# Attention products of 128 output channels issued as two column halves of 64, in a float32 stack of attentions and scans

## Chip, core and metric
The kernel runs on one NeuronCore of one Trainium2 chip. The metric is the device time of one execution in microseconds (us), inputs and output in device memory.

## What is computed
The input x is 4 images of 512 channels on 16 x 16 positions, float32. Four layers follow each other, each added to its own input; the input of a layer is group-normalised first (32 groups of 16 channels).

```python
# layers 0 and 2: attention over the 256 positions of an image
e1 = relu(w1 @ xf + b1); e2 = relu(w2 @ xf + b2)          # 64 channels each
assembly = relu(w3 @ xf + b3)                             # 512 channels
attn = softmax(e1.T @ e2)                                 # 256 x 256
y = alpha * (xf @ attn.T) + assembly
# layer 1 (PReLU) and layer 3 (ReLU): a scan along one image axis, forth and back
cur = act(Wc @ prev + b) + x_i                            # Wc 512 x 512, 64 columns
...
x = x + layer(group_norm(x))
```

## The kernel before
The 512 channels lie as K = 4 chunks of 128 partitions. Everything is float32, apart from some bfloat16 products of zeros that keep TensorE's clock up. The program is written per engine, with semaphores by hand, so the order of the instructions in the code is the order on each engine.

**Attention** (`attention` in TensorE's program, line 309) goes through four images one after the other. For each image TensorE issues, in this order:
- the embeddings of both branches at once (L330): 4 products, weights 128 x 128, on the 256 positions;
- in layer 2 only, 8 transposes of the normalised image, 128 x 128 (L338);
- the ReLU branch `relu_branch` (L318), output chunk m = 0 (and one product of m = 1 in layer 0), 4 products a chunk;
- the scores (L353): 2 products with 64 rows each, one on the lower and one on the upper 64 rows of the array;
- in the first and in the last image of an attention the product for group means of the norm to come (L299), behind the scores;
- the ReLU branch's chunk 1, then in the first and last image the product for group variances (L306), then chunk 2 (and one product of chunk 3 in layer 0);
- 4 transposes of the probabilities (L370), and the rest of the ReLU branch's chunk 3;
- the output (L383): 8 products, weights 128 x 128, on 256 positions, two for each output chunk.

ScalarE makes the embeddings (L467, L469), the exponentials and the ReLU branch's results out of the PSUM banks; VectorE finds the maximum, scales the probabilities, adds the residual (L668 or L671) and writes the new image (L685 or L688), and takes its statistics (L580). The three kinds of waits ahead of products are for embeddings (L350), probabilities (L367) and copied transposes (L379).

**Scans** (`scan_step`, L397) have 30 steps each. In a step 16 products of 128 x 128 weights go on 64 columns; each is issued as two products of 64 output channels (TILE = 64, L408), the first with its output on PSUM partitions 0 to 63 and the second on 64 to 127. Outside the scans, all weights with 128 output channels are used whole.

Around an attention, `critical_norm` (L437) issues the products of zeros (L290) and the group products while VectorE and GpSimd work out the norm.

Of the kernel before, what the change touches and what calls it, by code (L numbers as in the profile page):

```python
# [20 lines left out]
P = 128  # L21
N = 4
C = 512
K = C // P
T = 16
POS = T * T
PC = POS // P
# [25 lines left out]
TILE = 64  # L53
# [66 lines left out]
def preact_stack(nc, a):  # L120
    with ExitStack() as ctx:
        def sb(name, shape, dt=F32):
            return ctx.enter_context(nc.sbuf_tensor(name, shape, dt))
# [5 lines left out]
        bank = [banks[:, b] for b in range(8)]  # L129
# [10 lines left out]
        w12 = {l: sb(f"w12_{l}", [P, K, 2 * D]) for l in (0, 2)}  # L140
        w3 = {l: sb(f"w3_{l}", [P, K, C]) for l in (0, 2)}
# [22 lines left out]
        xn = [sb(f"xn{s}", [P, K, POS]) for s in range(2)]  # L164
# [5 lines left out]
        probT = sb("probT", [P, PC, POS])  # L170
# [71 lines left out]
        def images(engine, image):  # L242
            image(0, 0, first=True)
            with engine.Fori(0, (N - 2) // 2) as pair:
                image(pair * 2 + 1, 1)
                image(pair * 2 + 2, 0)
            image(N - 1, 1, last=True)
# [3 lines left out]
        def o_bank(m):  # L251
            return bank[(4, 7, 5, 6)[m]][:, 0:POS]
# [33 lines left out]
        def _(pe):  # L286
# [6 lines left out]
            def group_means(l, r):  # L293
                s = norm[l]
                c0, c1 = norm_rounds(l)[r]
                pe.wait_ge(s.stats, c1)
                if l == 0 and r == 0:
                    pe.wait_ge(s_gavg, 16)
                nc.tensor.matmul(bank[4][:, 0:(c1 - c0) * SETS], gavg[:], st[:, c0:c1, :, 1],  # L299
                                 start=True, stop=True).then_inc(s.mean, 1)  # L300

            def group_variances(l, r):
                s = norm[l]
                c0, c1 = norm_rounds(l)[r]
                pe.wait_ge(s.vadd, r + 1)
                nc.tensor.matmul(bank[5][:, 0:(c1 - c0) * SETS], gavg[:], vadd[:, c0:c1],  # L306
                                 start=True, stop=True).then_inc(s.var, 1)

            def attention(l):
                s = att[l]  # L310
                if l == 0:
                    pe.wait_ge(s_w12[l], 16)
                else:
                    pe.wait_ge(s_signed12, K)

                def relu_branch(xn_s, m, done, ks=range(K)):
                    for k in ks:
                        mm = nc.tensor.matmul(bank[2 + m // 2][:, m % 2 * POS:(m % 2 + 1) * POS],  # L318
                                              w3[l][:, k, m * P:(m + 1) * P], xn_s[:, k],
                                              start=(k == 0), stop=(k == K - 1))  # L320
                    if done:
                        mm.then_inc(s.a_mm, 1)

                if l == 0:
                    pe.wait_ge(s_small, 32)

                def image(n, h, first=False, last=False):
                    for k in range(K):
                        pe.wait_ge(s.xn_ready, n * K + k + 1)
                        mm = nc.tensor.matmul(bank[1][:, 0:POS], w12[l][:, k], xn[h][:, k],  # L330
                                              start=(k == 0), stop=(k == K - 1))
                    mm.then_inc(s.e_mm, 1)
                    if not first:
                        pe.wait_ge(s.x_done, n * K)
                    if l == 2:
                        for pc in range(PC):
                            for k in range(K):
                                mm = nc.tensor.transpose(bank[6 + pc][:, k * P:(k + 1) * P],  # L338
                                                         xn[h][:, k, pc * P:(pc + 1) * P], ident[:])
                            mm.then_inc(s.xnT_mm, 1)  # L340
                    if first:
                        if l == 0:
                            pe.wait_ge(s_w3[l], 16)
                        else:
                            pe.wait_ge(s_signed3, K)

                    ahead = 1 if l == 0 else 0
                    relu_branch(xn[h], 0, False)
                    relu_branch(xn[h], 1, False, range(ahead))
                    pe.wait_ge(s.e_ready, (n + 1) * 4)  # L350
                    for ic in range(PC):
                        rows = slice(ic * D, (ic + 1) * D)
                        mm = nc.tensor.matmul(scores[:, ic * POS:(ic + 1) * POS],  # L353
                                              e1[rows, ic * P:(ic + 1) * P], e2[rows], start=True, stop=True)
                    mm.then_inc(s.s_mm, 1)
                    if first:
                        group_means(l, 1)
                    if last:
                        group_means(l + 1, 0)
                    relu_branch(xn[h], 1, True, range(ahead, K))  # L360
                    if first:
                        group_variances(l, 1)
                    if last:
                        group_variances(l + 1, 0)
                    relu_branch(xn[h], 2, False)
                    relu_branch(xn[h], 3, False, range(ahead))
                    pe.wait_ge(s.p_ready, (n + 1) * PC)  # L367
                    for jc in range(PC):
                        for ic in range(PC):
                            mm = nc.tensor.transpose(bank[1 - jc][:, ic * P:(ic + 1) * P],  # L370
                                                     prob[:, ic, jc * P:(jc + 1) * P], ident[:])
                        mm.then_inc(s.pt_mm, 1)
                    relu_branch(xn[h], 3, True, range(ahead, K))
                    if l == 0:
                        pe.wait_ge(s_xT[n], 16)
                    else:
                        pe.wait_ge(s.xnT_copied, (n + 1) * PC)

                    pe.wait_ge(s.pt_copied, (n + 1) * PC)  # L379
                    by_position = xT[:, n] if l == 0 else xnT  # L380
                    for m in range(K):
                        for jc in range(PC):
                            mm = nc.tensor.matmul(o_bank(m),  # L383
                                                  by_position[:, jc, m * P:(m + 1) * P], probT[:, jc],
                                                  start=(jc == 0), stop=(jc == PC - 1))
                        mm.then_inc(s.o_mm, 1)
                        if m == 1:
                            pe.wait_ge(s.r_ready, (n + 1) * K)

                if l == 0:  # L390
                    for n in range(N):
                        image(n, n % 2, first=n == 0, last=n == N - 1)
                else:
                    images(pe, image)
# [50 lines left out]
            for l in range(0, 4, 2):  # L445
                critical_norm(l, 0)
                attention(l)
                critical_norm(l + 1, 1)
                if l == 0:
                    clear_banks()  # L450
                    prelu_scan()
                else:
                    relu_scan()
# [555 lines left out]
```

## Time and profile before

| | us |
|---|---|
| median of 3 runs | 268.09 |
| lowest, highest | 267.37, 268.49 |
| the profiled execution | 268.07 |
| its span, first to last instruction | 266.3 |
| TensorE matmul busy | 255.9 (96%) |
| TensorE weight load busy | 220.5 (83%) |
| VectorE busy | 174.6 (66%) |
| ScalarE busy | 94.2 (35%) |
| GpSimd busy | 66.2 (25%) |

The first attention runs from about 10 to 67 us of the span, the first scan from 72 to 139, the second attention from 145 to 202 and the second scan from 207 to 264. PE is TensorE's matmul, PEld its weight load, which can run beside it. Matmuls are pipelined, so the mean duration of one is longer than the distance between two; the busy time of a group of back-to-back matmuls, divided by their number, gives the distance. A float32 product shows as two MATMUL and two LDWEIGHTS records, each called a pass here.

### The profile page before, as it was taken

The page shows a single profiled execution, that of the slowest core. Times are in us where ns is not written, and L with a number is a line of the kernel's source. Part 1 is how long each engine was busy: PE and PEld are TensorE (multiplying, and loading weights), DVE is VectorE, ACT ScalarE, POOL GpSimd, SP SyncE. Part 2 cuts the span into 40 slices and gives each one's busy share as a digit, 9 for nine tenths or more (in the row PEclk, how much of TensorE's full clock was granted, in tenths as well). Part 3 has the DMA queues.
Part 4 walks back from the last instruction along what each step waited for, and adds up shares of the span by engine and source line. Part 5 has one row for each costly group of instructions (what it writes and reads, how often), then busy time and mean ns, then how long its engine had stood idle before and what let it go on. Part 6 is the DMA issues. An engine that isn't in the chain of part 4 may idle for free.

```text
span 266.3 us, 10980 instructions
## 1 busy us (share of the span) xinstructions
PE 255.9 (96%) x4480; PEld 220.5 (83%) x4480; DVE 174.6 (66%) x656; ACT 94.2 (35%) x225; POOL 66.2 (25%) x100
## 2 busy tenths in 40 slices
PE   8799999999879999999998999999998999999995
PEld 3578887878579999999984888888885899999995
DVE  2886666676887777777778763655568655555553
ACT  2054545445663333333320655637349200000000
POOL 0209200004232222333332030000040533334342
PEclk9799999999999999999999999999999999999999
DMA  6998000000000000000000000000000000002122
GB/s 212 402 417 333 0 0 0 4 0 0 1 5 0 0 0 0 1 0 0 0 0 1 2 0 0 4 0 0 0 2 1 2 0 0 0 20 79 59 79 79
DMA packets 5055, 11.34 MB, mean 43 GB/s; under 512 B 688, under 2 KB 3120, under 8 KB 4528
## 3 DMA queue, kind: packets, MB, share of 16 engines
q1 hardware_dynamic: 4752, 10.63, 10.5%
q10 hardware_dynamic: 288, 0.52, 0.6%
q8 instruction: 8, 0.13, 0.2%
q14 instruction: 7, 0.06, 0.1%
HBM read 9.05 MB, written 2.10 MB: 42 GB/s over the span
## 4 chain that ended last, share of the span: by engine, by line
PE 88%; DVE 8%; issue 2%; POOL 1%; ACT 0%; DVEq 0%; POOLq 0%
PE banks L409 45%; PE banks L318 20%; PE banks L383 8%; PE banks L330 6%; PE banks L290 2%; PE banks L353 2%; DVE st L580 1%; PE banks L370 1%; PE banks L338 1%; PE banks L306 1%; POOL rstd L897 1%; PE banks L299 1%; DVE xw L685 1%; DVE sloped L766 1%; DVE xh L688 1%
## 5 line engine op out<-in xcount | busy, mean ns | idle before, releaser
L409 PE MATMUL banks<-state,wc 128*64 128x64 f32 x3840 | 121.7, 224 | 2.1 <-DVE state L771 1.5
L409 PEld LDWEIGHTS banks<-state,wc 128*64 128x64 f32 x3840 | 117.1, 138 | 7.1 <-issue 2.0
L318 PE MATMUL banks<-xn,w 128*128 128x256 f32 x256 | 61.0, 384 | 0.0
L318 PEld LDWEIGHTS banks<-xn,w 128*128 128x128 f32 x256 | 46.7, 191 | 7.0 <-issue 1.3
L749 DVE SCALAR_TENSOR_TENSOR state<-banks,negb,inb 128x64 f32<-128x64 f32 x116 | 29.1, 281 | 24.1 <-PE banks L409 24.0
L897 POOL TENSOR_TENSOR rstd<-gvar,mhalf 128x2 f32<-128x2 f32 (+1 forms) x12 | 15.5, 1297 | 116.1 <-DVE gvar L613 116.1
L766 DVE SCALAR_TENSOR_TENSOR sloped<-banks,par,share 128x64 f32<-128x64 f32 x116 | 27.5, 279 | 16.0 <-PE banks L409 16.0
L771 DVE SCALAR_TENSOR_TENSOR state<-sloped,bent,banks 128x64 f32<-128x64 f32 x112 | 26.0, 274 | 0.0
L532 ACT COPY banks<-inb 128x256 f32 (+1 forms) x29 | 10.9, 376 | 37.3 <-DVE state L771 35.2
L467 ACT ACTIVATE e<-banks,par 64x256 f32<-64x256 f32 x16 | 7.5, 469 | 41.6 <-PE banks L330 41.4
L330 PE MATMUL banks<-xn,w 128*128 128x256 f32 x64 | 17.0, 413 | 1.8 <-DVE xn L624 1.8
L290 PE MATMUL banks<-zeros 128*128 128x512 bf16 x60 | 17.5, 431 | 1.2 <-DVE zeros L862 1.2
L330 PEld LDWEIGHTS banks<-xn,w 128*128 128x128 f32 x64 | 13.1, 207 | 4.6 <-issue 2.7
L938 POOL TENSOR_TENSOR xw<-xw,state 128x256 f32 (+1 forms) x15 | 11.0, 731 | 21.8 <-DVE state L771 21.8
L501 ACT ACTIVATE rel<-banks,par 128x256 f32<-128x256 f32 x32 | 13.3, 470 | 5.4 <-PE banks L318 5.4
L938 POOL TENSOR_TENSOR xh<-xh,state 128x256 f32 (+1 forms) x15 | 10.9, 729 | 17.1 <-DVE state L749 17.1
L533 ACT ACTIVATE share<-inb,oma 128x256 f32 (+1 forms) x30 | 15.1, 504 | 0.0
L383 PE MATMUL banks<-probT,xT 128*128 128x256 f32 x64 | 14.8, 382 | 0.0
L383 PE MATMUL banks<-probT,xnT 128*128 128x256 f32 x64 | 14.5, 379 | 0.0
L932 POOL TENSOR_TENSOR inb<-state,signb 128x256 f32 x14 | 8.6, 613 | 21.8 <-DVE state L771 21.8
L671 DVE SCALAR_TENSOR_TENSOR rx<-xw,sign,rel 128x256 f32<-128x256 f32 x16 | 9.1, 644 | 7.4 <-ACT rel L501 7.4
L383 PEld LDWEIGHTS banks<-probT,xT 128*128 128x128 f32 x64 | 12.0, 190 | 2.2 <-ACT rel L501 0.6
(84 smaller groups left out, 227.0 us busy)
## 6 DMA issues: line engine op xcount, KB each, us to landing
w<-in_w SPq DMA_DIRECT2D x2, 1024.0 KB, 11.5
xT<-in_xT SPq DMA_DIRECT2D x4, 512.0 KB, 11.0
wc<-in_wc SPq DMA_DIRECT2D x2, 1024.0 KB, 16.0
result<-xh SPq DMA_DIRECT2D x15, 128.0 KB, 1.8
x<-in_x SPq DMA_DIRECT2D x3, 512.0 KB, 8.5
x<-in_x ACTq DMA_DIRECT2D x1, 256.0 KB, 4.3
x<-in_x SPq DMA_DIRECT2D x1, 256.0 KB, 4.2
w<-in_w ACTq DMA_DIRECT2D x1, 256.0 KB, 4.7
```

What stands on the lines that cost most here:

```text
L290: nc.tensor.matmul(bank[b], zeros[:, 0:P], zeros[:], start=True, stop=True)
L318: mm = nc.tensor.matmul(bank[2 + m // 2][:, m % 2 * POS:(m % 2 + 1) * POS], w3[l][:, k, m * P:(m + 1) * P], xn_s[:, k], start=(k == 0), st ...
L330: mm = nc.tensor.matmul(bank[1][:, 0:POS], w12[l][:, k], xn[h][:, k], start=(k == 0), stop=(k == K - 1))
L383: mm = nc.tensor.matmul(o_bank(m), by_position[:, jc, m * P:(m + 1) * P], probT[:, jc], start=(jc == 0), stop=(jc == PC - 1))
L409: mm = nc.tensor.matmul(bank[K * h + m][c:c + TILE, 0:COLS], wc[l][:, k, m * P + c:m * P + c + TILE], state[:, h, k], start=first and not ...
L501: nc.scalar.activation(rel[:, m], bank[2 + m // 2][:, m % 2 * POS:(m % 2 + 1) * POS], ACT.Relu, bias=par[:, b3 + m:b3 + m + 1]).then_inc(s ...
L533: nc.scalar.activation(share[:, h], inb[:, t], ACT.Identity, scale=oma[:, 0:1]).then_inc(s.share, 1)
L749: nc.vector.scalar_tensor_tensor(new_state(q, h)[:, k], product(k, h), negb[:, k:k + 1], inb[:, t, k], ALU.max, ALU.add)\
L766: nc.vector.scalar_tensor_tensor(sloped[:, k], summed(q, k, h), par[:, PA_1:PA_1 + 1], share[:, h, k], ALU.mult, ALU.add).then_inc(s.slope ...
L771: nc.vector.scalar_tensor_tensor(new_state(q, h)[:, k], sloped[:, k], bent[:, k:k + 1], summed(q, k, h), ALU.add, ALU.max)\
L897: nc.gpsimd.tensor_tensor(rstd[:, c:c + width], gvar[:, c:c + width], mhalf[:, c:c + width], ALU.pow).then_inc(s.rstd, 1)
L938: nc.gpsimd.tensor_tensor(xr[:, t], xr[:, t], state[:, h], ALU.add).then_inc(s.taken, 1)
```

## The change
A helper `halves` issues a product as two, each with 64 of the 128 output channels: weights' columns 0 to 63 into PSUM partitions 0 to 63, then 64 to 127 into 64 to 127, both on the same 256 positions. It takes the place of the single product in the ReLU branch (L318), the embeddings (L330) and the output (L383). Transposes, scores, group products and scans stay.

```diff
+            def halves(out, w, v, start, stop):
+                for c in range(0, P, TILE):
+                    mm = nc.tensor.matmul(out[c:c + TILE], w[:, c:c + TILE], v, start=start, stop=stop,
+                                          skip_group_check=True)
+                return mm
+
...
-                        mm = nc.tensor.matmul(bank[2 + m // 2][:, m % 2 * POS:(m % 2 + 1) * POS],
-                                              w3[l][:, k, m * P:(m + 1) * P], xn_s[:, k],
-                                              start=(k == 0), stop=(k == K - 1))
+                        mm = halves(bank[2 + m // 2][:, m % 2 * POS:(m % 2 + 1) * POS],
+                                    w3[l][:, k, m * P:(m + 1) * P], xn_s[:, k], k == 0, k == K - 1)
...
-                        mm = nc.tensor.matmul(bank[1][:, 0:POS], w12[l][:, k], xn[h][:, k],
-                                              start=(k == 0), stop=(k == K - 1))
+                        mm = halves(bank[1][:, 0:POS], w12[l][:, k], xn[h][:, k], k == 0, k == K - 1)
...
-                            mm = nc.tensor.matmul(o_bank(m),
-                                                  by_position[:, jc, m * P:(m + 1) * P], probT[:, jc],
-                                                  start=(jc == 0), stop=(jc == PC - 1))
+                            mm = halves(o_bank(m), by_position[:, jc, m * P:(m + 1) * P], probT[:, jc],
+                                        jc == 0, jc == PC - 1)
```

## Rows read from the trace of the kernel before
**Rows 1.** The page: TensorE's matmuls and granted clock in 40 slices.
```profile
PE   8799999999879999999998999999998999999995
...
PEclk9799999999999999999999999999999999999999
```
**Rows 2.** The chain that ended last, in order of time: start us, us, what.
```profile
26.01 1.73 PE banks L330 x8
27.74 2.16 PE banks L318 x10
29.90 0.63 PE banks L353 x4
30.53 3.65 PE banks L318 x16
34.18 0.44 PE banks L370 x4
...
156.14 3.45 PE banks L383 x16
159.59 1.73 PE banks L330 x8
161.32 0.87 PE banks L338 x8
...
170.37 3.45 PE banks L383 x16
173.82 1.73 PE banks L330 x8
...
197.55 1.74 PE banks L318 x8
...
199.32 0.48 ACT rel L501
```
**Rows 3.** Windows of middle images: window, length, PE, PEld, DVE, ACT, POOL busy (count), clock, DMA.
```profile
26.00:39.50 13.50, 13.50 (x66) 11.13 (x65) 8.72 (x22) 6.69 (x17) 2.43 (x3) 1.00 0.00 0
...
159.60:173.80 14.20, 14.20 (x73) 12.04 (x73) 7.74 (x19) 7.46 (x18) 0.00 (x0) 1.00 0.01 2
```
**Rows 4.** Groups by line and shape: out<-in, shapes, count | busy us, mean ns | idle before.
```profile
L318 PE MATMUL banks<-xn,w 128*128 128x256 f32 x256 | 61.0, 384 | 0.0
...
L330 PE MATMUL banks<-xn,w 128*128 128x256 f32 x64 | 17.0, 413 | 1.8 <-DVE xn L624 1.8
L383 PE MATMUL banks<-probT,xT 128*128 128x256 f32 x64 | 14.8, 382 | 0.0
L383 PE MATMUL banks<-probT,xnT 128*128 128x256 f32 x64 | 14.5, 379 | 0.0
...
L409 PEld LDWEIGHTS banks<-state,wc 128*64 128x64 f32 x3840 | 117.1, 138 | 7.1 <-issue 2.0 <-DVE state L722 0.8 <-DVE state L771 0.2
...
L383 PEld LDWEIGHTS banks<-probT,xT 128*128 128x128 f32 x64 | 12.0, 190 | 2.2 <-ACT rel L501 0.6
...
L370 PEld LDWEIGHTS banks<-ident,prob 128*128 128x128 f32 x32 | 4.0, 141 | 0.8
```
**Rows 5.** The chain in the second scan.
```profile
207.94 55.69 PE banks L409 x1900
```
**Rows 6.** Timelines of ScalarE and TensorE around the scores of image 1, second attention.
```profile
162.84 0.47 ACT L469 ACTIVATE e<-banks,par 64x256 f32<-64x256 f32 x1
...
163.85 0.70 PE L353 MATMUL banks<-e 64*128 64x256 f32 x4
```
**Rows 7.** Timelines of TensorE around the variance products: start us, us, line, shape, count.
```profile
57.84 1.54 PE L318 MATMUL banks<-xn,w 128*128 128x256 f32 x6
59.48 0.40 PE L306 MATMUL banks<-vadd,gavg 128*128 128x24 f32 x2
...
150.05 1.97 PE L318 MATMUL banks<-xn,w 128*128 128x256 f32 x8
151.86 0.30 PE L306 MATMUL banks<-vadd,gavg 128*128 128x24 f32 x2
```
## The prediction
> **What bounds the kernel now.** I began with the page's busy shares and slices [rows 1]. TensorE is busy 96% of the span and its slices read 9 nearly everywhere, so an edit to its products can count; the granted clock reads 9 from the third slice on. Next came the chain that ended last, for one middle image of each attention and for the end of the last image [rows 2]. In a middle image the chain is TensorE alone, from the embedding products (L330) to the attention output (L383): 13.5 us an image in the first attention and 14.2 us in the second. Whatever TensorE loses there, the kernel loses. At the end of an attention the chain leaves TensorE after the last ReLU-branch products (L318) and goes over ScalarE into VectorE, so the last image's 16 output passes lie beside it. The windows show the other engines' slack: in such an image VectorE is busy 7.74 to 8.72 us and ScalarE 6.69 to 7.46 us [rows 3].
>
> **What a product costs.** The groups by shape [rows 4] give 256 passes at L318 for 128 products, 64 at L330 for 32 and 128 at L383 for 64: an f32 product is two passes. The chain's 16 passes in 3.45 us and 8 in 1.73 us [rows 2] make a pass of 256 columns 216 ns. A transpose of 128 columns takes 0.87 / 8 = 109 ns. The difference is 107 ns for 128 columns, 0.836 ns a column, and 2 ns are fixed. The weight load is hidden under this stream: LDWEIGHTS means are 190 ns for 128 output channels, 141 ns for the transposes and 138 ns for 64 output channels [rows 4], so 64 f32 channels less shorten a load by 52 ns, and 128 take about 104 ns, under 216. The change shortens something that costs nothing while the stream runs.
>
> **Term 1, the passes.** Each of 448 passes becomes two, one per column half. The scans already run such pairs: 1900 passes in 55.69 us [rows 5] are 29.3 ns each, 58.6 ns a pair on 64 columns. Sixty-four columns at 0.836 ns are 53.5 ns. So the halves stream together, and a pair has 5.1 ns fixed where a full pass has 2. On 256 columns I take 214 + 5 = 219 ns a pair, +3 ns. Of the 448 passes, 2 x 16 lie beside the chain; 416 x 3 ns = 1.2 us.
>
> Bounds: at worst the whole 58.6 ns grows with the columns, 234 ns a pair, +18 ns, 7.5 us. At best the pair at 64 columns is held up by its loads (also about 52 ns), and the halves stream faster than the full array does; at half the time, 112 ns, this is a large gain (rival 2). I take 219 because the pairs of row halves at the scores, also 256 columns, need the full array's 216 ns, as the next term finds, and because 53.5 ns fits 64 columns without anything new.
>
> In its page "TensorE: Matmul & The Clock Gate", section "Part 3: Packing small matmuls", the Trainium skill puts a second tile at about 4 ns of issue over the duration of one. By that the term would be 416 x 4 = 1.7 us; the scans' pair is 3 ns, so the trace nearly agrees.
>
> **Term 2, changes between tilings.** This is not in the diff's text, but in what stands between the changed products. The scores (L353) use 64 rows for one product and the other 64 rows for the second. Their four passes take 0.63 us in the chain [rows 2]. Streaming as two pairs they need 0.43, so going in costs 0.20 us. Coming out, the 16 passes of L318 take 3.65 us where 16 of L383 take 3.45: again 0.20. It is no wait for data: in the second attention ScalarE has written the last embedding at 163.31, and the scores start at 163.85 [rows 6]. Some 0.10 of the 0.20 is a load nobody hides, the rest an emptying engine. By contrast, transposes between full products cost nothing: 0.44 us for four is their stream [rows 2].
>
> After the change, transposes and group products stay on the full array amid column-tiled neighbours. The trace of before has no such passage without idle time around it, so its cost is bounded: 0 if only row tiles empty the array, 0.20 if it is like L353. I take the latter less the shorter load: 0.15 us into column halves or into transposes, 0.20 into a full f32 product. Per image:
> - First attention, images 1 and 2: scores to column halves 0.15 where it was 0.20, into the transposes (L370) 0.15, out 0.15: +0.25 each.
> - First attention, images 0 and 3: in and out of L370, 0.30, and out of the variance product (L306), 0.15: +0.45 each. In from L299 and into L306 would be 0.35, but TensorE stands still there: six passes from 57.84 are done streaming at 59.14, and L306 starts at 59.48 [rows 7]. That 0.34 covers them.
> - Second attention, images 1 and 2: four passages around L338 and L370, 0.60, less 0.05: +0.55 each.
> - Second attention, images 0 and 3: these four, and L299 to L318 0.15, L318 to L306 0.20, L306 to L318 0.15: 1.10. Idle time covers only 0.08 here (eight passes from 150.05 end at 151.78, L306 starts at 151.86 [rows 7]): about +1.0 each.
>
> Together 2 x (0.25 + 0.45 + 0.55 + 1.0) = 4.5 us.
>
> The Trainium skill's page "TensorEngine Tiling (Array Packing)", under "Key Properties", says that a change of tiling mode, unlike one of tile, drains the engine. That rule speaks against this change and gives the 4.5 us; without it the term is about -0.2. The row-tiled scores agree, at 0.20 us a passage; for column tiles no run here shows it.
>
> **Costed at nothing:** twice the instructions (the scans issue one pass per 29 ns, here 110 ns are to be had), and the scans and copies, which the diff leaves alone. The first pass after a real stall may start 0.05 us sooner by the shorter load; it has one instance per attention and is dropped.
>
> **The sum.** 268.07 (profiled execution: span 266.3 and 1.8 around it) + 4.5 + 1.2 = 273.8 us. The median of the runs is 268.09, so no shift. That is 2.1% slower.
>
> **Rivals.**
> 1. *Column halves don't empty the array.* Only the passages at L353 are seen to cost anything, and they separate row tiles. Then 1.2 us and a few shorter loads (four of 0.05): 269.1 us. For it: no row shows the other case. Against: the passage costs the same both ways at L353, so the full array needs emptying as much as the row tiles do.
> 2. *Faster, by the halves' stream.* Decides if a half streams faster than the full array, which the scans' 58.6 ns can't exclude since the loads are as long. At 112 ns a pair a middle image loses 56 x 104 ns = 5.8 us, but VectorE's up to 8.7 us of work become its floor: images of about 9 us in place of 13.6 and 14.2, some 4.6 and 5.2 less, and about 4 less in each end image. 2 x 4.6 + 2 x 5.2 + 4 x 4 = 36; near 232 us. Against: row halves on 256 columns run at the full array's pace. The Trainium skill's page "TensorE: Matmul & The Clock Gate", section "Back-to-back issue gap", gives N/2.4 + 2.5 ns, 109 ns for 256 columns; the f32 passes here take 216, so the trace disagrees.
> 3. *Worse.* Pairs at the proportional 234 ns: 7.5 + 4.5, 280 us. Against it is the good fit of 53.5 ns.
>
> **Chances.** The forecast 0.77, rival 1 0.13, rival 2 0.05, rival 3 0.05. About 0.5% (1.3 us) is what can be told from no change; rival 1 lies within it. So faster 0.05, same 0.13, slower 0.82. The range must hold rival 1 and the costs of the forecast: low 269.0; high with some 32 passages at the full 0.20, 6.4 + 1.2 = 7.6, so 276.0 rounded up.
>
> **What would show it.** Right: 896 passes of 64 channels on 256 columns in place of 448; LDWEIGHTS there near 138 ns; 16 pairs of L383's work in 3.50 us; middle images of 13.9 and 14.9 us; about 0.15 us of idle time in the weight loads before each L338, L370, L299 and L306 and behind each; scans unchanged. Wrong: four transposes still in 0.44 us between column halves (rival 1), pairs well under 216 ns (2) or near 234 (3).

## The result, and the profile after

| | before | after |
|---|---|---|
| median of 4 runs, us | 268.09 | 272.11 |
| the profiled execution, us | 268.07 | 272.06 |
| its span, us | 266.3 | 270.3 |
| TensorE matmul passes | 4480 | 4928 |

The changed kernel is slower: the ratio is 1.0151, 95% interval 1.0132 to 1.0169, or 4.0 us. The forecast was 273.8 us.

The changed kernel's groups by shape (the helper's line is L312; out<-in, shapes, count, busy us, mean ns) answer to [rows 4]:

```profile
L312 PE MATMUL banks<-xn,w 128*64 128x256 f32 x640 | 77.5, 390 | 1.8 <-DVE xn L628 1.8
...
L312 PE MATMUL banks<-probT,xT 128*64 128x256 f32 x128 | 14.5, 379 | 0.0
L312 PE MATMUL banks<-probT,xnT 128*64 128x256 f32 x128 | 14.5, 379 | 0.0
...
L312 PEld LDWEIGHTS banks<-probT,xnT 128*64 128x64 f32 x128 | 9.2, 137 | 4.6
```

All 896 passes are there, with loads of 137 ns where they were 190, but the output groups are busy for 14.5 us with 128 passes each, and were for 14.8 and 14.5 us with 64 [rows 4]. So two halves stream in the time of one whole pass.

The chain that ended last, from the scores of image 1 to those of image 2, in the first and then in the second attention (start us, us, what), answers to [rows 2]:

```profile
30.45 0.63 PE banks L358 x4
31.08 3.60 PE banks L312 x32
34.68 0.58 PE banks L375 x4
35.27 8.80 PE banks L312 x80
44.07 0.63 PE banks L358 x4
...
166.15 0.63 PE banks L358 x4
166.78 3.60 PE banks L312 x32
170.38 0.59 PE banks L375 x4
170.97 7.06 PE banks L312 x64
178.03 1.02 PE banks L343 x8
179.05 1.88 PE banks L312 x16
180.93 0.63 PE banks L358 x4
```

The scores (now L358) still take 0.63 us. The four transposes (L375) take 0.59 in place of 0.44, the eight (L343) 1.02 in place of 0.87, and each stretch of column halves behind them 0.15 above 216 ns a pair: 1.88 for 8 pairs, 7.06 for 32. Behind the scores it is 3.60 in place of 3.65. From scores to scores an image of the second attention takes 14.78 us, 0.55 more than the 14.23 of before; one of the first takes 13.62, only 0.05 more than 13.57. For the second attention before:

```profile
163.92 0.63 PE banks L353 x4
178.15 0.63 PE banks L353 x4
```

Between the first embeddings and ScalarE's last ReLU results the second attention grew from 54.65 to 57.57 us (+2.92), and the first, counted from its first variance product, from 45.72 to 46.58 (+0.86). These are 3.8 of the 4.0 us. The rest lies in the start of the program, where the first embeddings begin at 10.12 in place of 9.89; that place varied between 9.55 and 10.35 in the profiles of the kernels here. The scans are the same to 0.01 us.

The weight loads around the transposes show the two passages (the bracket is idle time ahead of the group):

```profile
34.61 0.42 PEld L375 LDWEIGHTS banks<-ident,prob 128*128 128x128 f32 x4 [0.39 <-issue]
35.20 0.84 PEld L312 LDWEIGHTS banks<-xn,w 128*64 128x64 f32 x10 [0.17 <-issue]
```

Nothing in the profile releases these loads ("issue"). The idle time of the loads, 0.39 and 0.17 us, is not the price of a passage, since part of it lies under a running stream; the prediction had expected about 0.15 in both places. Before, the transposes' loads began while the product ahead was still streaming, with no idle time in front of them (the transposes themselves start at 34.18 in the chain):

```profile
34.02 0.36 PEld L370 LDWEIGHTS banks<-ident,prob 128*128 128x128 f32 x3
```

### The profile page after: what moved, and what is told of

It reads as the page before. It is cut to its first block, busy times and chain, and to the rows that moved or that the text cites. A ratio compares the mean times of both kernels' runs of the same rounds, so it can differ in the third digit from the quotient of the medians.

```text
span 270.3 us, 11876 instructions
## 1 busy us (share of the span) xinstructions
PE 260.2 (96%) x4928; PEld 199.9 (74%) x4928; DVE 174.4 (65%) x656; ACT 94.1 (35%) x225; POOL 66.1 (24%) x100
## 4 chain that ended last, share of the span: by engine, by line
PE 89%; DVE 7%; issue 2%; POOL 1%; ACT 0%; DVEq 0%; POOLq 0%
PE banks L413 45%; PE banks L312 35%; PE banks L290 2%; PE banks L358 2%; PE banks L375 2%; PE banks L343 2%; DVE st L584 1%; PE banks L306 1%; PE banks L299 1%; POOL rstd L901 1%; DVE xw L689 1%; DVE sloped L770 1%; DVE xh L692 1%; DVE rx L675 0%; ACT rel L505 0%
## 5 line engine op out<-in xcount | busy, mean ns | idle before, releaser
L312 PE MATMUL banks<-xn,w 128*64 128x256 f32 x640 | 77.5, 390 | 1.8 <-DVE xn L628 1.8
L312 PEld LDWEIGHTS banks<-xn,w 128*64 128x64 f32 x640 | 45.2, 139 | 25.9 <-issue 6.0
L312 PE MATMUL banks<-probT,xT 128*64 128x256 f32 x128 | 14.5, 379 | 0.0
L312 PE MATMUL banks<-probT,xnT 128*64 128x256 f32 x128 | 14.5, 379 | 0.0
L645 DVE TENSOR_REDUCE mx<-banks 128x2 f32<-128x512 f32 x8 | 5.5, 692 | 11.2 <-PE banks L358 11.2
L584 DVE BATCH_NORM_STATS2 st<-xw 128x6 f32<-128x256 f32 x32 | 12.3, 420 | 0.6
L312 PEld LDWEIGHTS banks<-probT,xnT 128*64 128x64 f32 x128 | 9.2, 137 | 4.6
```

What stands on the lines that cost most here:

```text
L312: mm = nc.tensor.matmul(out[c:c + TILE], w[:, c:c + TILE], v, start=start, stop=stop, skip_group_check=True)
L584: nc.vector.bn_stats(st[:, n * K + k].rearrange("p a b -> p (a b)"), src).then_inc(norm[l].stats, 1)
```

## Experiments

Two readings of the 4.0 us were to be told apart first. A passage is a place in TensorE's queue where the tiling changes. **A**: each passage between the full array and column halves costs a fixed time. "Before beside it" is the kernel before, run again next to each experiment. **B**: the cost goes with the number of doubled passes.

### Parts of the change, and many more passages

```diff
 # relu_only: L330 and L383 whole again; embed_out_only: L318 whole again
 # alternate: only the ReLU branch, odd k in halves
+                        product = halves if k % 2 else whole
+                        mm = product(bank[2 + m // 2][:, m % 2 * POS:(m % 2 + 1) * POS],
+                                     w3[l][:, k, m * P:(m + 1) * P], xn_s[:, k], k == 0, k == K - 1)
```

> Only the ReLU branch in column halves; embeddings and output are whole products as before. Theory A (each passage between the full array and column halves costs 0.15 us into halves or transposes and 0.20 us into a whole f32 product, passes cost the same 216 ns): per middle image of the second attention L343 to ReLU 0.15, scores to ReLU -0.05, transposes 0.15 and 0.15, ReLU to output 0.20 = +0.60 us; end images about +1.0; first attention about +0.4 in middle images, 0.6 to 0.8 in end ones: +5.4 us against before, which is MORE than the whole change's +4.0. Theory B (the cost goes with the number of doubled passes, 4.0 us over 448 passes = 9 ns each): 256 passes, +2.3 us.

> Only embeddings and attention output in column halves. Theory A: output to next embeddings needs no passage; into the output 0.15 us, embeddings to whole ReLU products 0.20 us (first attention; 0.15 us of it under ScalarE in middle images), embeddings to transposes 0.15 us (second attention): about +2.0 us against before. Theory B (9 ns for each of 192 doubled passes): +1.7 us. Tells little by its total; the idle places in the weight loads should be at just these two places.

> ReLU branch alone, odd k in column halves and even k whole, so nearly every product changes the tiling. Theory A: 7 or 8 passages of 0.15 us and 7 or 8 of 0.20 us per image, about 2.6 us an image, +20 us against before. Theory B (9 ns for each of 128 doubled passes): +1.1 us. Rival C (a passage costs only beside transposes and row tiles, not between two kinds of plain product): about +1 us.

| | doubled passes | median, us | before beside it | ratio (95%) |
|---|---|---|---|---|
| relu_only | 256 | 273.10 | 268.11 | 1.0195 (1.0164 to 1.0226) |
| embed_out_only | 192 | 269.58 | 268.11 | 1.0063 (1.0038 to 1.0088) |
| alternate | 128 | 287.53 | 268.11 | 1.0713 (1.0675 to 1.0751) |

The kernel with the fewest doubled passes is the slowest by far, and the ReLU branch alone (+5.0 us) costs more than the whole change. B, which had said +2.3 and +1.1 us for these two, is out. A had said +5.4, +2.0 and +20 us; +5.0, +1.5 and +19.4 were measured. The total of embed_out_only alone fits B's +1.7 as well; its middle images in the second attention show the two passages, 14.53 us in place of 14.23. Image by image, relu_only's middle images take 14.83 and 13.96 us (+0.60 and +0.39, expected 0.60 and about 0.4). The chain of alternate shows both prices side by side:

```profile
183.39 0.58 PE banks L312 x4
183.97 0.63 PE banks L317 x2
184.60 0.58 PE banks L312 x4
185.19 3.65 PE banks L393 x16
```

Two pairs of halves or two whole passes stream in 0.43 us. With a passage ahead they take 0.58 and 0.63: 0.15 into halves, 0.20 into whole products, between plain products with no transpose or wait between them. Rival C (only beside transposes and row tiles) falls too.

### All in columns but the scores

```diff
-                            mm = nc.tensor.transpose(bank[1 - jc][:, ic * P:(ic + 1) * P],
-                                                     prob[:, ic, jc * P:(jc + 1) * P], ident[:])
+                            mm = halves(bank[1 - jc][:, ic * P:(ic + 1) * P],
+                                        prob[:, ic, jc * P:(jc + 1) * P], ident[:], True, True)
...
+                halves(bank[5][:, 0:(c1 - c0) * SETS], gavg[:], vadd[:, c0:c1], True, True).then_inc(s.var, 1)
```

> The changed kernel with group products in column halves too, and the transposes as plain products with the identity in column halves (two passes in place of one), so that only the row-tiled scores change the tiling. Theory A: no idle weight-load time around transposes; four transposes take 0.87 us and eight 1.74 us with no passage, against 0.44 + 0.30 and 0.87 + 0.30 with them; second attention +1.26 us an image against before, first attention +0.2 to +0.4: +6 us against before, +2 against the changed kernel. If passages cost something other than emptying (the semaphore waits that stand there), the gaps stay: +8 to +10 us.

Group means and the eight transposes of the normalised image are changed in the same way. Measured: 273.21 us beside 268.11, ratio 1.0185 (1.0156 to 1.0214), +5.1 us where +6 were expected.

```profile
166.50 0.63 PE banks L356 x4
167.13 14.86 PE banks L295 x160
181.99 0.63 PE banks L356 x4
```

In the second attention 15.49 us from scores to scores, +1.26 against before, as expected to the hundredth: twelve transposes as two passes each, 12 x 0.109 = 1.31, less 0.05 for the shorter load behind the scores. The stretch of 160 records has a timeline row for its transposes:

```profile
162.86 1.92 PE L295 MATMUL banks<-ident,xn 128*64 128x128 f32 x32
164.60 0.60 PE L295 MATMUL banks<-xn,w 128*64 128x256 f32 x4
```

Sixteen pairs of 128 columns start within 1.74 us, 109 ns each, and nothing stands idle around them, although the same waits for probabilities and embeddings stand in the code. So the gaps are not those waits. Leaving the transposes on the full array, gaps and all, is still the cheaper way.

### The scores without row tiles

```diff
-                        rows = slice(ic * D, (ic + 1) * D)
                         mm = nc.tensor.matmul(scores[:, ic * POS:(ic + 1) * POS],
-                                              e1[rows, ic * P:(ic + 1) * P], e2[rows], start=True, stop=True)
+                                e1[:, ic * P:(ic + 1) * P], e2[:], start=True, stop=True)
...
-                    for rows in (slice(0, D), slice(D, 2 * D)):
+                    for rows in (slice(0, D),):
...
+            for e in (e1, e2):
+                nc.vector.memset(e[D:2 * D], 0.0).then_inc(s_zeros, 1)
```

This is scores_whole, made from the kernel before. scores_halves is the changed kernel with the same scores, each issued through `halves`.

> The kernel before with the scores as two products on all 128 rows, the lower half of embeddings zero, so that nothing changes the tiling inside an attention (ScalarE writes two embeddings an image in place of four). Theory A: the four passes go one after the other, 0.86 us, where the two row halves took 0.43 and the two passages 0.20 each; 8 x 0.03 = +0.2 us, no visible difference, and the 16 passes behind the scores take 3.45 us, not 3.65. If those 0.20 were something else than passages (a wait on ScalarE's embeddings), they stay: 8 x 0.43 = +3.4 us, or with the wait alone removed less.

> The changed kernel with the scores on 128 rows in column halves, so no row tile is left, while transposes and group products stay on the full array. Theory A: 0.86 us in place of 0.43 + 0.20 + 0.15, so +0.08 us an image, +0.7 us against the changed kernel, +4.7 against before; no gap around the scores.

scores_whole: 268.80 us beside 268.46, ratio 1.0004 (0.9988 to 1.0021).

```profile
178.91 0.86 PE banks L353 x4
179.77 3.45 PE banks L318 x16
```

The 16 passes behind the scores take 3.45 us, so the 0.20 went with the tiling, and the scores' own stream takes it back: an image of 14.26 us in place of 14.23. scores_halves: 272.71 us, ratio 1.0165 (1.0144 to 1.0187) to before, +4.25 us where +4.7 were expected; its image takes 14.86 us, 0.08 above the changed kernel's 14.78, as expected.

### Halves to quarters

```diff
-            def halves(out, w, v, start, stop):
-                for c in range(0, P, TILE):
+            def halves(out, w, v, start, stop, tile=TILE):
+                for c in range(0, P, tile):
...
-                                    w3[l][:, k, m * P:(m + 1) * P], xn_s[:, k], k == 0, k == K - 1)
+                                    w3[l][:, k, m * P:(m + 1) * P], xn_s[:, k], k == 0, k == K - 1,
+                                    TILE // 2 if m == 2 else TILE)
```

> The changed kernel with chunk 2 of the ReLU branch in column quarters (32 output channels, four to a product). Theory A1: a change between halves and quarters empties the array like one between the full array and halves: 0.12 us in and 0.15 out, +0.27 us an image, +2.2 us against the changed kernel, +6.2 against before. Theory A2: only leaving or entering the full array or row tiles does: 0 against the changed kernel. Four passes of 32 channels on 256 columns take 216 ns together if they stream at the same time, as the halves do.

Measured: 272.65 us beside 268.46, ratio 1.0168 (1.0145 to 1.0191). The total is 0.5 us above the changed kernel's, between A1's +2.2 and A2's 0, and by itself decides nothing. The stretch between scores and transposes does, in the first and in the second attention:

```profile
30.67 3.89 PE banks L312 x48
...
167.09 3.74 PE banks L312 x48
```

It holds the same 16 slots of 216 ns as the 3.60 us in the changed kernel. In the second attention it has one change of size, +0.14, and in the first, where one product of chunk 3 follows, two, +0.29. A1 is right in its price. The expectation miscounted the places: in the second attention the way out of the quarters leads into the transposes, where a passage stood anyway. Counted rightly it is about 1.1 us, and that is what the two attentions grew by (47.43 and 57.82 us where the changed kernel has 46.58 and 57.57, counted as above); the profiled execution's start was 0.5 us shorter. Four quarters need the slot of one whole pass.

### Why the first attention paid less: ScalarE's order

Before the change the 16 output passes took 3.63 us in the first attention's middle images and 3.45 in the second's. In these images the wait at L388 held TensorE for 0.18 us. It is for ReLU results that ScalarE writes after normalising the next image, and it is missing from the three kinds of waits named at the head of the document. The chain, and the weight load that waited:

```profile
35.91 3.63 PE banks L383 x16
...
37.55 1.59 PEld L383 LDWEIGHTS banks<-probT,xT 128*128 128x128 f32 x8 [0.31 <-ACT rel L501]
```

```diff
                             nc.scalar.copy(by_rows(l, probT[:, 0]), in_order(l, bank[1][:, 0:POS])).then_inc(s.pt_copied, 1)
-                            if not last and not first:
-                                normalise_next()
                             act.wait_ge(s.a_mm, n * 2 + 2)
...
-                    if first:
+                    if not last:
                         normalise_next()
```

> The kernel before with ScalarE's normalising of the next image moved behind the last two ReLU results. In the first attention's middle images TensorE waits 0.18 us ahead of the third output chunk for these results (L388). Theory A: that wait goes, the middle images take 13.37 us in place of 13.57, -0.4 us in all. If the wait is something else: no change.

> The same move in the changed kernel. Theory A: the passages there have already eaten the wait (middle image 13.60 of TensorE's own work in 13.62), so nothing is gained, 0 to -0.1 us; the change then costs 0.3 to 0.4 us more against its own reordered kernel of before than the 4.0 measured. Rival: the wait is still there in full, -0.4 us.

before_order: 267.35 us beside 268.27, ratio 0.9970 (0.9955 to 0.9985): faster than both kernels. Its chain:

```profile
34.28 1.30 PE banks L318 x6
35.58 3.45 PE banks L383 x16
```

Two middle images went from 13.57 to 13.36, which is 0.4 us; of the other 0.5 the profile shows 0.3 in the start of the program, which varies anyway, so only the 0.4 is put down to the order. after_order: 271.76 us, ratio 1.0124 (1.0103 to 1.0144) to before; its middle images take 13.61 us where they took 13.62. So in the changed kernel the passages had used up that wait, and with the wait gone from both the change costs 271.76 - 267.35 = 4.4 us. The totals are too uncertain to tell 4.4 from 4.0, but the stage does: the first attention, counted as above, takes 45.31 us in before_order and 46.54 in after_order, +1.23 where it was +0.86.

> before_order and scores_whole together. Theory A: the sum of the two, -0.4 (the wait) + 0.2 = -0.2 us or up to the -0.9 measured for before_order alone + 0.2. A gain beyond before_order would mean that ScalarE's two dropped embeddings are worth something on the path.

Measured: 268.29 us, ratio 1.0001 (0.9987 to 1.0015). The two dropped embeddings are worth nothing on the path. It is 0.5 us below scores_whole's 268.80, too little for the totals to confirm before_order's gain. Its chain does: 13.39 us from scores to scores in the first attention, where scores_whole has 13.60.

### What is fixed in a slot

```diff
-TILE = 64
+TILE = 32
```

> The kernel before with the scans' products in column quarters of 32 output channels (TILE = 32) in place of halves; attention as it was. The pass term of the prediction assumed a fixed 5 ns in a pair of halves, but on 256 and on 128 columns a pair now shows 2.4 ns above its stream, and only the scans' 64 columns show 5. Theory L: on 64 columns the weight load of 64 channels (about 53 ns and what is fixed with it) is the longer of the two, so shorter loads bring a slot from 58.3 to 55.8 ns: 1920 slots x 2.5 ns = -4.8 us. Theory F: the 5 ns is the issue of several records, which grows with four of them: 58.3 to 60 ns or more, 0 to +10 us. Attention unchanged in both.

> scan_quarters and before_order together: the scans' change of the run beside it, and -0.4 to -0.9 us for ScalarE's order.

scan_quarters: 273.70 us beside 268.30, ratio 1.0201 (1.0176 to 1.0226). The total lies in Theory F's range, and Theory L's -4.8 us fails; yet the slot does what Theory L says, and not what F says. order_quarters: 273.39 us, ratio 1.0184 (1.0153 to 1.0214), 0.3 us below scan_quarters, which is within the noise. Windows of 0.5 and 2.5 us from the same start in the second scan, quarters first, then the kernel before:

```profile
228.50:229.00 0.50, 0.50 (x51) 1.00 0.00 0
228.50:231.00 2.50, 2.50 (x194) 1.00 0.00 0
```

```profile
228.00:228.50 0.50, 0.50 (x25) 1.00 0.00 0
228.00:230.50 2.50, 2.50 (x94) 1.00 0.00 0
```

In 2 us there are 143 / 4 = 35.8 slots with quarters, 55.9 ns each, and 69 / 2 = 34.5 with halves, 58.0 ns. The loss is elsewhere (chain, and one body's weight loads):

```profile
211.21 2.73 PE banks L409 x171
213.94 1.47 issue
215.40 0.87 PE banks L409 x45
216.27 0.05 issue
216.31 3.78 PE banks L409 x256
220.09 0.05 issue
...
220.14 3.62 PEld L409 LDWEIGHTS banks<-state,wc 128*32 128x32 f32 x256 [0.21 <-issue]
```

Once through the loop's body takes 3.83 us where 64 slots of 55.9 ns are 3.58: the loads of a body run for 3.62 us and stand idle for 0.21 between two bodies. With halves 64 slots took 3.75 us (58.6 ns each [rows 5]), with no such gap. In the first scan there was nothing to gain, as a slot took 67.9 ns there with halves, well above either load or stream:

```profile
75.57 30.44 PE banks L409 x896
```

Theory L's sum had counted those slots too. And at some places TensorE stands for 1.2 to 1.7 us with nothing in the profile to wait for: once here, and at 78.90 and 82.28 in the first scan. Its idle time put down to "issue" in this group is 5.9 us, against none that showed before; order_quarters has the same three standstills, at 1.0 to 1.4 us. With quarters an instruction covers half the time. What holds TensorE there wasn't tried and stays open.

## Why the prediction was right, and where it was off

**Term 2, right in mechanism and price.** The step "0.15 us into column halves or into transposes, 0.20 us into a full f32 product" holds at every place: 0.59 - 0.44, 1.02 - 0.87, 1.88 - 1.73, and both prices in alternate's chain. The range of 269.0 to 276.0 us held rival 1 as well, so it is these places and not the total that decide. The price is an emptying of some 0.10 us and the next load, about 0.05 us for 64 channels (or for a transpose) and 0.10 for 128. That the first part is the engine's emptying is inferred from the idle places, their size and their absence wherever the tiling stays; the profile has no record of it.

The Trainium skill's "TensorEngine Tiling (Array Packing)", "Key Properties", says that a change of mode drains the engine. No row of before could show it for column tiles; these runs agree with it, at 0.15 to 0.20 us a passage, and 0.14 between halves and quarters.

**Its size, 3.8 us where the text had 4.5.** Middle images were to take 13.9 and 14.9 us and took 13.62 and 14.78. Two things were mis-sized.

The first is "First attention, images 1 and 2 ... +0.25 each": 0.05 to 0.07 was measured, which makes 0.4 of the 0.7 us. The text named idle time only at the variance products and missed that the middle images had 0.18 us of their own, between the transposes and the third output chunk. ScalarE starts that piece when the first transposes land, so the passage out of them was hidden by it. before_order and after_order show this. It could be read beforehand: 3.63 against 3.45 us for the same 16 passes.

The second is the 0.15 us for the way out of a group product, in the images 0 and 3 of both attentions. The eight ReLU passes behind one already took 1.82 us before, 0.09 above their 1.73, and take 1.88 now, so only 0.06 was new. In image 0 of the second attention, before and then after:

```profile
149.87 0.33 PE banks L299 x2
150.21 1.82 PE banks L318 x8
152.02 0.13 PE banks L306 x2
152.16 1.82 PE banks L318 x8
```

```profile
151.19 0.33 PE banks L299 x2
151.52 1.88 PE banks L312 x16
153.39 0.33 PE banks L306 x2
153.73 1.88 PE banks L312 x16
```

So these images grew by 0.37 us in the first attention and by 0.90 and 0.92 in the second, where the text had 0.45 and 1.0. That is the other 0.3 us; what the 0.09 of before consists of wasn't tried. The way into the variance product (L306) costs its full 0.20, from 0.13 to 0.33.

**Term 1, 0.0 us where the text had 1.2.** "214 + 5 = 219 ns a pair" is wrong; a pair takes 216, as a whole pass does, and so do four quarters. The 5 ns of the scans' pairs were carried from 64 columns to 256 as if every pair had them. On 128 columns a pair takes 109 ns, in line with 256, and on 64 columns quarters, with shorter loads, bring the slot down by 2 ns. So with 64 channels on 64 columns the load, estimated at 52 ns, is about as long as the stream of 53.5 and adds what is left; that it is the load and not something else that comes with its length is argued from this one slot. On 256 columns the load is far from that.

The Trainium skill's "TensorE: Matmul & The Clock Gate", "Part 3: Packing small matmuls", puts a second tile at about 4 ns. The halves' records do start some 6 ns apart (the changed kernel's trace at 172.03 and 172.25 us), but over a row of pairs (7.06 us for 32 with one passage of 0.15) nothing of it is left: the measurement decides, and it is under 1 ns a pair.

**The rest.** 268.07 + 3.8 + 0.2 at the start = 272.1. The two errors, 0.7 and 1.2 us, have the same sign and make up the distance to 273.8, less that 0.2. Rival 1 (only row tiles empty the array) falls by alternate, rival 2 (faster halves) and rival 3 (234 ns) by the 216 ns. The reason that there was nothing to gain stands as the text had it: on 256 columns the 128-channel load, about 104 ns, lies under a stream of 214, so a shorter load saves nothing while the stream runs. It saves 0.05 us where a stream begins anew, as behind the scores.

## What to carry to other kernels

Splitting a product's output channels over column tiles shortens the weight load, not the stream, and brings nothing on 256 float32 columns, where the load is already hidden. On 64 columns, where load and stream are about equal, quarters took 2 ns off the slot of halves, and lost it again around the loop; whole products on 64 columns weren't run. What counts is how often the tiling changes along TensorE's queue: count the passages in program order, whole to halves to rows and between sizes of tile, at 0.15 us plus the difference in the next load, and take off those that fall into idle time. If one kind of product stays on the full array amid the others, converting a part of the rest can cost more than converting all of it.

## Not expected

- A change of tile size within column tiling (64 to 32 channels) costs 0.14 us, as much as leaving the full array.
- Four passes of 32 channels on 256 columns run in the slot of one, 216 ns, with eight records in it (four loads, four matmuls); on 64 columns in 55.9 ns. But the scans with such short instructions showed standstills of 1.0 to 1.7 us that no wait explains, and made the faster slot worth nothing: +5.4 us in all.
- The two passages of 0.20 us around the row-tiled scores give back nearly all that running both row halves at once saves: 0.43 + 0.40 = 0.83 us, against 0.86 for scores on all rows.
